# A two-layer transformer kernel: inverse head norms by ten operations for each sequence, and all first-layer rounds ordered ahead of all second-layer rounds

## The chip, the cores and the metric

The kernel runs on one core of one Trainium2 chip. The metric is the time on the device in microseconds (us) for one execution; lower is better. Times of a kernel are given as the median of several runs.

## The reference

Two transformer layers work on 8 sequences of 128 tokens with 256 channels, conditioned by one vector of 256 for each sequence.

```python
# first layer: 16 heads of 16
ada = silu(cond) @ Wada.T + bada            # gamma1, gamma2, scale1, scale2, shift1, shift2
q, k, v = split((ln(x) * (scale1 + 1) + shift1) @ Wqkv.T + bias)
qn = q / max(norm(q), 1e-12) * exp(min(scale_mul_log, log(100)))
kn = k / max(norm(k), 1e-12)
x = x + (softmax(qn @ kn.T + mask) @ v @ Wproj.T + bproj) * gamma1
x = x + (gelu_tanh((ln(x) * (scale2 + 1) + shift2) @ Wfc1.T + bfc1) @ Wfc2.T + bfc2) * gamma2
# second layer: 8 query heads of 32, one key and value head, rotary positions
h = ada_rms(x, cond, ln1_w, ln1_tw)
x = x + softmax(rope(h @ Wq.T) @ rope(h @ Wk.T).T / sqrt(32)) @ (h @ Wv.T) @ Wo.T
h = ada_rms(x, cond, ln2_w, ln2_tw)
x = x + (silu(h @ Wg.T) * (h @ Wu.T)) @ Wd.T
```

The hidden width of both MLPs is 1024.

## The kernel before, in words

**Tiling.** A token is a partition. A round is one pair of sequences in one layer; there are 4 pairs and 2 layers, so 8 rounds, listed in `ROUNDS` (line 57) as (pair, layer). The step number `n` is twice the round plus the sequence within the pair, and `j = n % 2` picks one of two buffers. Each round has an attention part ("a") and an MLP part ("m"). Products with Wqkv, Wfc1, Wq, Wkv, Wg and Wu are made from high and low parts in three matmuls (lines 1366 to 1368); ScalarE (ACT) makes the high part of the activations (line 944) and GpSimd (POOL) the low part (line 822).

**A first-layer attention, for each sequence.** `norm_stats` (VectorE, DVE), `norm_root` (POOL), `norm_apply` (DVE), a transpose on TensorE (PE), `norm_mod` and `norm_high` (ACT), `norm_low` (POOL), `qk_product` (PE), `qk_copy` (DVE, line 1155), `qk_square` (ACT, line 952) and `qk_sum` (DVE: the sum at line 1175, the floor at line 1180, and a first guess of the inverse root from the bits at lines 1185 and 1188). Then `qk_root` on POOL (lines 826 to 848) refines the guess, once for both sequences of the pair: one operation for minus half of the sum, three Newton steps of four operations on 128x64 values, and one that multiplies the q half by the head scale (line 847), 14 operations in all. `qk_scale` (DVE, line 1195) multiplies q and k by the result, `qk_high` (ACT, lines 960 and 961) and `qk_low` (POOL, lines 854 and 855) split them into half-precision parts, and `q_turn` and `k_turn` (PE, lines 1443 and 1452) transpose them, with copies on DVE. Four groups of four heads follow: `scores` (PE, line 1481), `mask_add` and `row_max` (DVE, lines 1254 and 1265), `exp` (ACT, line 980), `probs_turn` (PE, line 1497), `probs_copy` (ACT, line 1000), `values` (PE, line 1513). At the end stand `project` (PE, line 1532), `residual` (DVE, line 1308) and `residual_add` (POOL, line 884 times gamma, line 887 plus x).

**The rest.** A second-layer attention has two groups for each sequence (exp at line 984), normalised on POOL (line 874). A first-layer MLP has four chunks `fc1` (two sums on ACT at line 1019, then lines 1024, 1315, 1031 and 1324) and two `down` products (line 1562); a second-layer MLP has eight chunks `gate_up` with little ACT work and the same two `down` products.

**Order.** Nothing in the file lists the instructions. At build time `list_steps` writes each step with its engine, an assumed duration, what it comes after, and a priority put together from `ATT_BASE`, `MLP_BASE`, `SHIFT` and others; `make_orders` then plays these steps through with a greedy rule and so fixes the order in each engine's queue and the PSUM banks. An engine works its queue strictly in that order and waits where a semaphore isn't there yet. Where the plan sees PE idle, it puts in filler matmuls (`warm`, line 1396) that keep TensorE's clock up; they compute nothing. There is one PSUM bank for transposes ("turn"), one for linear products, two for hidden ones. Steps of one kind follow `n`: the norms, scores, projections and MLPs of a round come after those of the rounds ahead of it in `ROUNDS`; different kinds can overlap, so an MLP of one round runs beside the attention of another.

**Gammas.** The gammas of a pair go through a scratch tensor in memory and are loaded back by SyncE (line 777) into one of two buffers (pair % 2). The load for pair 2 waits until the first-layer MLP residual of pair 0 has been scaled, and that for pair 3 until that of pair 1 has been (line 884 releases it). `residual_add` on POOL waits for the gammas of its pair.

Of the kernel before, what the change touches and what calls it, by code (L numbers as in the profile page):

```python
# [28 lines left out]
ALU = mybir.AluOpType  # L29
# [3 lines left out]
P = 128  # L33
# [10 lines left out]
MAX_LOG_SCALE = float(np.log(np.float32(100.0)))  # L44
GELU_C = float(np.sqrt(2.0 / np.pi).astype(np.float32))
# [4 lines left out]
NEWTON = 3  # L50
# [24 lines left out]
for _i, _c in enumerate(CHUNKS):  # L75
# [14 lines left out]
SHIFT = {  # L90
    'warm': 900.0, 'angles': 925.5, 'attn_copy': 434.0, 'cond_silu': -640.5, 'cond_tanh': -405.5, 'down':
    947.5, 'exp': 360.0, 'fc1': -277.0, 'gamma_load': -658.5, 'gamma_store': 624.5, 'gate': -299.0,
    'gate_up': 365.5, 'gelu': -1217.0, 'gelu_in': 1213.0, 'gelu_inner': 16.5, 'head_clip': 1045.5,
    'head_exp': 500.5, 'inv_copy': 16.5, 'inv_spread': 490.5, 'inv_turn': 90.0, 'k_copy': -524.0, 'k_turn':
    -1072.5, 'load': -193.0, 'load_small': 627.0, 'load_whole': 1282.0, 'load_x': -159.5, 'mask_add':
    -171.0, 'modulate': 747.0, 'modulated': 9.5, 'norm_apply': -1665.5, 'norm_high': -1020.5, 'norm_low':
    -756.0, 'norm_mod': -339.0, 'norm_probs': -148.0, 'norm_root': 55.0, 'norm_stats': -323.5, 'norm_turn':
    -635.5, 'probs_copy': 382.0, 'probs_turn': -90.0, 'project': -100.0, 'q_copy': 132.0, 'q_turn': 98.0,
    'qk1_copy': 629.0, 'qk1_turn': -1542.5, 'qk_copy': 291.0, 'qk_high': 218.5, 'qk_low': -419.0,
    'qk_product': -509.5, 'qk_root': -297.5, 'qk_scale': -261.0, 'qk_square': -313.0, 'qk_sum': 49.0,  # L100
    'qkv1_copy': -1082.5, 'qkv1_product': 401.0, 'residual': -48.0, 'residual_add': 119.0, 'rope': 1132.5,
    'row_inverse': 1112.5, 'row_max': -1805.5, 'scores': -397.0, 'sines': 391.5, 'store': 1349.0,
    'sum_inverse': -962.0, 'tanh': -19.5, 'v_copy': -307.0, 'v_product': 1260.5, 'values': -69.5,
    'weight_high': 592.0, 'weight_low': 626.0, ('norm_stats', 'a'): 285.5, ('norm_stats', 'm'): -665.0,
    ('norm_root', 'a'): 136.0, ('norm_root', 'm'): -1064.0, ('norm_apply', 'a'): -644.5, ('norm_apply',
    'm'): -450.5, ('norm_turn', 'a'): -712.5, ('norm_turn', 'm'): 265.5, ('norm_mod', 'a'): -873.0,
    ('norm_mod', 'm'): 40.0, ('norm_high', 'a'): -363.0, ('norm_high', 'm'): -559.0, ('norm_low', 'a'):
    -278.5, ('norm_low', 'm'): 436.5, ('residual', 'a'): -248.5, ('residual', 'm'): -49.0, ('residual_add',
    'a'): 1035.0, ('residual_add', 'm'): 113.0}
# [17 lines left out]
LATENCY = 2.2  # L127
# [26 lines left out]
def list_steps():  # L154
# [39 lines left out]
    for i, name in enumerate(WHOLE):  # L194
        add(("load_whole", name), "SP", 0.75 if i < 2 else 3.0, [], at=0.0)
# [35 lines left out]
    for r, (pair, layer) in enumerate(ROUNDS):  # L231
# [4 lines left out]
        for j, n in enumerate(ns):  # L236
# [5 lines left out]
            if layer == 0:  # L242
                w_ready = ("weight_low", CHUNK_AT[("Wqkv", 2)])
                add(("qk_product", n), "PE", 1.55, [("norm_low", "a", n), w_ready], "linear", at=a)
# [3 lines left out]
                add(("v_product", n), "PE", 0.8, [("norm_low", "a", n), ("qk_product", n), ("weight_low", LAST_CHUNK["Wqkv"])], "linear", at=a + 0.1)  # L248
# [4 lines left out]
                if j == 1:  # L253
                    add(("qk_root", r), "Pool", 5.0, [("qk_sum", m) for m in ns] + [("head_exp",)], at=a)
                for m in ns if j == 1 else ():
                    b = base + 2 + 1.0 * (m % 2)
                    add(("qk_scale", m), "DVE", 0.6, [("qk_root", r)], at=b)
                    add(("qk_high", m), "ACT", 0.85, [("qk_scale", m), last_j.get(("kt", m % 2))], at=b)
                    add(("qk_low", m), "Pool", 1.75, [("qk_high", m)], at=b)
                    add(("q_turn", m), "PE", 0.53, [("qk_low", m)], "turn", at=b)  # L260
                    add(("q_copy", m), "DVE", 0.665, [("q_turn", m), last_scores], frees=("q_turn", m), at=b)
                    add(("k_turn", m), "PE", 0.25, [("q_turn", m)], "turn", at=b)
                    add(("k_copy", m), "DVE", 0.33, [("k_turn", m), last_scores], frees=("k_turn", m), at=b)
                    last_j[("qk", m % 2)], last_j[("pack", m % 2)], last_j[("kt", m % 2)] = (("qk_scale", m), ("qk_low", m),
                                                                                          ("k_turn", m))
            else:
                add(("qkv1_product", n), "PE", 1.0, [("norm_low", "a", n), ("weight_low", LAST_CHUNK["Wkv"])],
# [5 lines left out]
                add(("qk1_turn", n), "PE", 0.43, [("rope", n)], "turn", at=a)  # L273
# [33 lines left out]
            if layer == 0:  # L307
# [41 lines left out]
        for j, n in enumerate(ns):  # L349
# [4 lines left out]
                + ([("gamma_load", pair)] if layer == 0 else [])  # L354
# [132 lines left out]
def build(nc, x, columns, pos, mask, w, out):  # L487
    with ExitStack() as ctx:
# [52 lines left out]
        head_scale = sb("head_scale", [P, H0])  # L541
# [23 lines left out]
        qk_half = sb("qk_half", [P, 2, 2 * H0])  # L565
# [229 lines left out]
        def _(pool):  # L795
# [4 lines left out]
            pool.memset(minus_half[:, :], -0.5)  # L800
            pool.memset(v_pad[:, :, :, :], 0.0)
# [24 lines left out]
            def qk_root_(r):  # L826


                o = ord0(2 * r) // 2
                half, t, y = qk_half[:, :, :], qk_t[:, :, :], qk_r[:, :, :]  # L830
                done = o * 4 * NEWTON
                pool.wait_ge(qk_guess, 2 * o + 2)
                pool.tensor_scalar(half, qk_fl[:, :, :], -0.5, None, ALU.mult)
                for i in range(NEWTON):
                    if i:
                        pool.wait_ge(qk_root_step, done + 4 * i)
                    pool.tensor_tensor(t, y, y, ALU.mult).then_inc(qk_root_step, 1)
                    pool.wait_ge(qk_root_step, done + 4 * i + 1)
                    pool.tensor_tensor(t, t, half, ALU.mult).then_inc(qk_root_step, 1)
                    pool.wait_ge(qk_root_step, done + 4 * i + 2)  # L840
                    pool.tensor_scalar(t, t, 1.5, None, ALU.add).then_inc(qk_root_step, 1)
                    pool.wait_ge(qk_root_step, done + 4 * i + 3)
                    pool.tensor_tensor(y, y, t, ALU.mult).then_inc(qk_root_step, 1)
                pool.wait_ge(qk_root_step, done + 4 * NEWTON)
                if o == 0:
                    pool.wait_ge(scale_ready, 1)
                pool.tensor_tensor(qk_r[:, :, 0:H0], qk_r[:, :, 0:H0],
                                   head_scale[:, :].unsqueeze(1).to_broadcast([P, 2, H0]), ALU.mult).then_inc(qk_rnorm, 1)
# [768 lines left out]
```

## Time and profile before

| what | us |
|---|---|
| median of 3 runs (lowest, highest) | 340.05 (339.28, 344.35) |
| the profiled execution, its whole time | 337.69 |
| its span, first to last instruction | 335.9 |
| mean granted clock of TensorE in it | 0.98 of full speed |

The profile is of one execution. A group of instructions is named by its line in the kernel's file, its engine and its operation. "Busy" is the time in which an engine had an instruction under way; busy time of PE holds the filler matmuls too. "Idle before" is the time in which the engine stood still ahead of these instructions, with the instruction whose end released it.

### The profile page before, as it was taken

The page shows a single profiled execution, that of the slowest core. Times are in us where ns is not written, and L with a number is a line of the kernel's source. Part 1 is how long each engine was busy: PE and PEld are TensorE (multiplying, and loading weights), DVE is VectorE, ACT ScalarE, POOL GpSimd, SP SyncE. Part 2 cuts the span into 40 slices and gives each one's busy share as a digit, 9 for nine tenths or more (in the row PEclk, how much of TensorE's full clock was granted, in tenths as well). Part 3 has the DMA queues.
Part 4 walks back from the last instruction along what each step waited for, and adds up shares of the span by engine and source line. Part 5 has one row for each costly group of instructions (what it writes and reads, how often), then busy time and mean ns, then how long its engine had stood idle before and what let it go on. Part 6 is the DMA issues. An engine that isn't in the chain of part 4 may idle for free.

```text
span 335.9 us, 7317 instructions
## 1 busy us (share of the span) xinstructions
PE 301.0 (90%) x2516; PEld 251.2 (75%) x2516; DVE 221.2 (66%) x535; ACT 207.0 (62%) x698; POOL 149.7 (45%) x264
## 2 busy tenths in 40 slices
PE   7797766799987989986999999999979999999986
PEld 7396555576866866765797878889768898988985
DVE  3854788688777889858868688664453883543441
ACT  3454639989992899887699576836571433632110
POOL 3446959764475453688325138522214512202000
PEclk9599999999997999999999999999979999999999
DMA  6998223000000020000001000000000000000000
GB/s 200 283 338 283 83 92 126 1 2 3 1 2 2 0 65 0 3 1 3 0 2 64 0 2 2 2 0 18 8 12 0 2 0 18 17 2 19 16 0 33
DMA packets 14037, 14.30 MB, mean 43 GB/s; under 512 B 1569, under 2 KB 12961, under 8 KB 14001
## 3 DMA queue, kind: packets, MB, share of 16 engines
q1 hardware_dynamic: 14000, 13.83, 13.1%
q8 instruction: 21, 0.34, 0.4%
q14 instruction: 16, 0.12, 0.1%
HBM read 12.76 MB, written 1.06 MB: 41 GB/s over the span
## 4 chain that ended last, share of the span: by engine, by line
PE 54%; DVE 16%; POOL 9%; issue 8%; ACT 8%; DMA 3%; SPq 1%; DVEq 0%; POOLq 0%; ACTq 0%
PE ps_linear L1562 15%; PE ps_hidden L1366 6%; PE ps_hidden L1368 5%; PE ps_hidden L1367 5%; PE ps_linear L1532 3%; PE ps_probs L1497 3%; ACT z L980 3%; DMA stage<-in_Wqkv 3%; DVE z L1254 2%; PE ps_scores L1486 2%; PE ps_turn L1402 2%; DVE neg_max L1265 2%; PE ps_output L1513 2%; PE ps_turn L1396 1%; PE ps_scores L1481 1%
## 5 line engine op out<-in xcount | busy, mean ns | idle before, releaser
L980 ACT ACTIVATE z<-z,neg_max 128x128 f32<-128x128 f32 x128 | 49.6, 391 | 13.1 <-DVE neg_max L1265 12.9
L822 POOL TENSOR_TENSOR h_lo<-xn,h_hi 128x256 fp32r<-128x256 f32 x32 | 24.1, 756 | 40.9 <-ACT h_hi L944 40.8
L1000 ACT ACTIVATE probsT<-ps_probs 128x512 f32<-128x512 f32 x48 | 28.4, 591 | 11.3 <-PE ps_probs L1497 11.2
L1497 PE MATMUL ps_probs<-ident,z 128*128 128x128 f32 x192 | 29.9, 278 | 3.7 <-ACT probsT L1000 2.6
L1562 PE MATMUL ps_linear<-WdT,g_h 128*128 128x256 f32 x128 | 29.5, 383 | 1.4 <-DVE g_h L1337 1.3
L1036 ACT ACTIVATE g_a<-ps_hidden 128x256 f32<-128x256 f32 x32 | 12.4, 387 | 29.0 <-PE ps_hidden L1368 28.6
L874 POOL TENSOR_TENSOR z<-z,row_inv 128x512 f32<-128x512 f32 x16 | 17.0, 1062 | 28.1 <-DVE row_inv L1279 28.1
L1562 PE MATMUL ps_linear<-Wfc2T,g_h 128*128 128x256 f32 x128 | 29.4, 382 | 0.0
L1497 PEld LDWEIGHTS ps_probs<-ident,z 128*128 128x128 f32 x192 | 21.7, 141 | 7.7 <-ACT probsT L1000 3.7
L1562 PEld LDWEIGHTS ps_linear<-WdT,g_h 128*128 128x128 f32 x128 | 23.7, 190 | 5.0 <-issue 1.4
L984 ACT ACTIVATE z<-ps_scores,neg_max 128x128 f32<-128x128 f32 x64 | 22.6, 368 | 7.8 <-DVE neg_max L1271 7.8
L1562 PEld LDWEIGHTS ps_linear<-Wfc2T,g_h 128*128 128x128 f32 x128 | 23.8, 191 | 3.6 <-issue 0.2
L1254 DVE TENSOR_TENSOR z<-ps_scores,bias_mask 128x512 f32<-128x512 f32 x32 | 21.9, 683 | 5.1 <-PE ps_probs L1497 3.4
L884 POOL TENSOR_TENSOR res_t<-res_t,gamma 128x256 f32<-128x256 f32 x16 | 13.5, 846 | 24.9 <-DVE res_t L1308 24.9
L980 ACT ACTIVATION_READ_ACCUMULATOR z<-z,neg_max 128x1 f32 x128 | 24.2, 189 | 0.0
L1265 DVE TENSOR_REDUCE neg_max<-z 128x4 f32<-128x512 f32 x32 | 21.7, 679 | 1.1
L1332 DVE SCALAR_TENSOR_TENSOR g_b<-g_a,ps_hidden 128x256 f32<-128x256 f32 x32 | 13.4, 417 | 12.9 <-ACT g_a L1036 12.6
L1366 PE MATMUL ps_hidden<-h_hi,WgT_hi 128*128 128x256 f32 x64 | 21.0, 328 | 0.3 <-ACT g_u L1019 0.3
L1366 PE MATMUL ps_hidden<-h_hi,Wfc1T_hi 128*128 128x256 f32 x64 | 19.4, 302 | 0.0
L816 POOL TENSOR_TENSOR rstd<-msq,minus_half 128x1 f32<-128x1 f32 x32 | 18.1, 566 | 2.7
L1366 PE MATMUL ps_linear<-WqkvT_hi,h_hi 128*128 128x512 f32 (+1 forms) x32 | 12.3, 384 | 7.0 <-DVE qk L1155 2.9
L1366 PE MATMUL ps_hidden<-h_hi,WuT_hi 128*128 128x256 f32 x64 | 18.1, 283 | 0.0
(166 smaller groups left out, 897.5 us busy)
## 6 DMA issues: line engine op xcount, KB each, us to landing
gamma<-gamma_scratch SPq DMA_DIRECT2D x8, 256.0 KB, 3.8
stage<-in_Wada SPq DMA_DIRECT2D x6, 256.0 KB, 4.0
stage<-in_Wqkv SPq DMA_DIRECT2D x4, 256.0 KB, 4.9
X<-in_x SPq DMA_DIRECT2D x4, 256.0 KB, 5.3
stage<-in_Wfc SPq DMA_DIRECT2D x4, 256.0 KB, 5.8
Wfc2T<-in_Wfc SPq DMA_DIRECT2D x1, 1024.0 KB, 7.5
WdT<-in_Wd SPq DMA_DIRECT2D x1, 1024.0 KB, 8.5
stage<-in_Wg SPq DMA_DIRECT2D x4, 256.0 KB, 2.7
```

Source lines behind the costliest of these rows:

```text
L816: pool.tensor_tensor(rstd[:, k, :], msq[:, k, 1:2], minus_half[:, 0:1], ALU.pow).then_inc(rstd_ready[kind], 1)
L822: pool.tensor_tensor(h_lo[:, m, :, j * P:(j + 1) * P], h_full[:, m, j, :, :], h_hi[:, m, :, j * P:(j + 1) * P].bitcast(F32), ALU.subtract) ...
L874: pool.tensor_tensor(z[:, d, :, :], z[:, d, :, :], row_inv[:, d, :].unsqueeze(2).to_broadcast([P, 4, P]), ALU.mult).then_inc(probs_ready, 1)
L980: ins = act.activation(z[:, d, u, :], z[:, d, u, :], ACT.Exp, bias=neg_max[:, d, u:u + 1], accum_out=head_sum[:, n % 2, t, u, b:b + 1])
L984: ins = act.activation(z[:, d, u, :], ps_scores[u // 2][:, (u % 2) * P:(u % 2 + 1) * P], ACT.Exp, bias=neg_max[:, d, u:u + 1], accum_out=r ...
L1000: act.activation(probsT[:, G % 2, :, :], bank_of(key)[:, :].rearrange("p (u q) -> p u q", u=4), ACT.Copy).then_inc(is_freed(key)[0], 1)
L1254: ins = dve.tensor_tensor(z[:, G % DEEP, :, :], ps_scores[b][:, :].rearrange("p (u k) -> p u k", u=4), bias_mask[:, :].unsqueeze(1).to_bro ...
L1265: dve.tensor_reduce(neg_max[:, d, :], z[:, d, :, :], AX_X, ALU.max, negate=True).then_inc(max_ready, 1)
L1366: pe.matmul(dst, sh, mh, start=i == 0, stop=False)
L1367: pe.matmul(dst, sh, ml, start=False, stop=False)
L1497: ins = pe.transpose(bank[:, u * P:(u + 1) * P], z[:, G % DEEP, u, :], ident[:, :])
L1562: ins = pe.matmul(bank[:, 0:C], g_h[:, f, j * P:(j + 1) * P], WT1[name][:, f, :], start=(f == 0), stop=(f == FT - 1))
```

## The change

1. `ROUNDS` becomes all four first-layer rounds, then all four second-layer rounds; before, round 3 is the second layer of pair 0 and round 4 the first layer of pair 3.
2. `qk_root` runs once for each sequence on 128x32 values, in ten operations: one step of third order (six operations) and one Newton step (four). The head scale is folded in earlier: `head_exp` makes the exponential of minus twice the log scale, and the floor in `qk_sum` becomes one operation that also multiplies by it, so the inverse root comes out scaled. The buffer `qk_half` goes, `qk_u` comes.
3. The step list: assumed durations are other numbers, some steps come after other ones in the plan, every step of a kind comes after the one before it (a new loop at the end of `list_steps`), and all the priority numbers are others. So the order in every queue is another.

```diff
+MIN_LOG_SCALE = -20.0
-NEWTON = 3
-ROUNDS = [(0, 0), (1, 0), (2, 0), (0, 1), (3, 0), (1, 1), (2, 1), (3, 1)]
+ROUNDS = [(0, 0), (1, 0), (2, 0), (3, 0), (0, 1), (1, 1), (2, 1), (3, 1)]
...
-GROUP_US = [-39.5, -38.5]
-ATT_BASE = [-1173.0, 265.0, 221.5, -749.5, 36.5, 113.5, -2.0, 608.0]
-MLP_BASE = [58.5, 771.5, 12.5, -147.0, -1056.5, -973.5, -16.5, -206.0]
+GROUP_US = [-44.5, -668.5]
+ATT_BASE = [-4536.0, -432.5, 816.5, -3308.5, 363.5, -2581.0, 60.5, 745.5]
+MLP_BASE = [554.0, 3234.5, -2707.0, -1333.0, -1121.0, -4845.5, 1417.5, -1651.5]
...
-LATENCY = 2.2
+LATENCY = 3.0
...
-        add(("load", c), "SP", 0.75, [user] if c >= STAGE else [], at=due)
+        add(("load", c), "SP", 0.95, [user] if c >= STAGE else [], at=due)
...
-                add(("qk_sum", n), "DVE", 1.25, [("qk_square", n), last_j.get(("qk", j))], at=a)
+                add(("qk_sum", n), "DVE", 1.3, [("qk_square", n), ("head_exp",), last_j.get(("qk", j))], at=a)
+                add(("qk_root", n), "Pool", 3.5, [("qk_sum", n)], at=a)
+                add(("qk_scale", n), "DVE", 1.0, [("qk_root", n)], at=a)
...
-                    add(("qk_root", r), "Pool", 5.0, [("qk_sum", m) for m in ns] + [("head_exp",)], at=a)
...
-                    add(("qk_scale", m), "DVE", 0.6, [("qk_root", r)], at=b)
...
-            add(("project", n), "PE", 0.95, [("attn_copy", n), ("load_whole", "Wproj" if layer == 0 else "Wo"), prev(("project",), n)], "linear", at=g)
+            add(("project", n), "PE", 0.95, [("attn_copy", n), ("load_whole", "Wproj" if layer == 0 else "Wo"), prev(("project",), n)]
+                + ([("gamma_load", pair)] if layer == 0 else []), "linear", at=g)
...
+    last = {}
+    for key, step in steps.items():
+        name = key[:2] if len(key) > 2 and isinstance(key[1], str) else key[0]
+        if name not in ("load", "load_x", "load_whole", "gamma_load", "modulate", "modulated", "store"):
+            if name in last and last[name] not in step[2]:
+                step[2].append(last[name])
+            last[name] = key
...
+            pool.memset(head_scale[:, H0:2 * H0], 1.0)
...
+            def qk_root_(n):
+
+                o, j = ord0(n), n % 2
+                x, t, u, y = qk_fl[:, j, :], qk_t[:, j, :], qk_u[:, j, :], qk_r[:, j, :]
+                done = o * 9
+                pool.wait_ge(qk_guess, o + 1)
+                pool.tensor_tensor(t, y, y, ALU.mult).then_inc(qk_root_step, 1)
+                pool.wait_ge(qk_root_step, done + 1)
+                pool.tensor_tensor(t, t, x, ALU.mult).then_inc(qk_root_step, 1)
+                pool.wait_ge(qk_root_step, done + 2)
+                pool.tensor_scalar(u, t, 0.375, -1.25, ALU.mult, ALU.add).then_inc(qk_root_step, 1)
...
+                pool.tensor_tensor(y, y, t, ALU.mult).then_inc(qk_rnorm, 1)
...
-                act.activation(head_scale[:, :], head_log[:, :], ACT.Exp).then_inc(scale_ready, 1)
+                act.activation(head_scale[:, 0:H0], head_log[:, :], ACT.Exp, scale=-2.0).then_inc(scale_ready, 1)
...
-                    dve.wait_ge(qk_rnorm, o // 2)
-                dve.tensor_scalar(qk_fl[:, j, :], qk_ss[:, j, :], NORM_FLOOR, None, ALU.max).then_inc(qk_floored, 1)
+                    dve.wait_ge(qk_rnorm, o - 1)
+                if o == 0:
+                    dve.wait_ge(scale_ready, 1)
+                    dve.wait_ge(consts_set, 2)
+                dve.scalar_tensor_tensor(out=qk_fl[:, j, :], in0=qk_ss[:, j, :], scalar=NORM_FLOOR,
+                                         in1=head_scale[:, :], op0=ALU.max, op1=ALU.mult).then_inc(qk_floored, 1)
```

## Rows read from the trace of the kernel before

**Rows 1.** The page: busy time, and the span in 40 slices.

```profile
PE 301.0 (90%) x2516; PEld 251.2 (75%) x2516; DVE 221.2 (66%) x535; ACT 207.0 (62%) x698; POOL 149.7 (45%) x264
...
PE   7797766799987989986999999999979999999986
```

**Rows 2.** Busy time of every engine in five stretches (us, busy, and count).

```profile
core 0: us, PE busy (x) PEld busy (x) DVE busy (x) ACT busy (x) POOL busy (x), PEclk, DMA share, GB/s
0.00:80.00 80.00, 62.86 (x571) 50.61 (x572) 54.03 (x127) 51.63 (x165) 50.46 (x102) 0.96 0.48 148
80.00:140.00 60.00, 55.08 (x502) 42.48 (x501) 50.12 (x116) 49.35 (x179) 32.58 (x58) 0.97 0.04 11
140.00:200.00 60.00, 54.27 (x472) 45.65 (x470) 45.19 (x99) 46.70 (x155) 29.51 (x49) 1.00 0.03 10
200.00:300.00 100.00, 97.14 (x772) 83.53 (x771) 60.01 (x167) 53.83 (x189) 34.16 (x51) 0.98 0.02 7
300.00:336.00 36.00, 31.67 (x207) 28.89 (x206) 11.82 (x29) 5.53 (x15) 2.97 (x6) 1.00 0.05 16
```

**Rows 3.** The same stretches for the filler matmuls of line 1396 alone.

```profile
0.00:80.00 80.00, 25.00 (x174) 22.51 (x174) 0.96 0.48 148
80.00:140.00 60.00, 5.48 (x28) 4.56 (x28) 0.97 0.04 11
140.00:200.00 60.00, 3.79 (x22) 2.92 (x22) 1.00 0.03 10
200.00:300.00 100.00, 0.71 (x4) 0.52 (x4) 0.98 0.02 7
300.00:336.00 36.00, 4.86 (x32) 4.37 (x32) 1.00 0.05 16
```

**Rows 4.** Stretches from 49 us on: all engines (columns of rows 2), then line 980 alone.

```profile
49.00:136.00 87.00, 76.80 (x776) 59.52 (x776) 70.74 (x154) 75.79 (x286) 51.25 (x82) 0.98 0.06 19
...
49.00:136.00 87.00, 39.39 (x192) 0.98 0.06 19
136.00:163.00 27.00, 0.00 (x0) 1.00 0.01 2
163.00:200.00 37.00, 13.14 (x64) 1.00 0.05 16
```

**Rows 5.** Timeline from 24 to 41 us: start, us, instruction [idle before <-releaser].

```profile
24.06 0.18 DVE L1188 TENSOR_SCALAR qk_r<-qk_t 128x32 int32<-128x32 int32 x1
...
26.96 0.40 POOL L833 TENSOR_SCALAR qk_half<-qk_fl 128x64 f32<-128x64 f32 x1 [5.30 <-DVE qk_r L1188]
...
32.24 0.25 POOL L847 TENSOR_TENSOR qk_r<-qk_r,head_scale 128x32 f32<-128x32 f32 x1
...
32.52 2.90 DVE L1195 TENSOR_TENSOR qk_n<-qk,qk_r 128x512 f32<-128x512 f32 x2 [3.70 <-POOL qk_r L847]
...
40.07 0.82 DVE L1180 TENSOR_SCALAR qk_fl<-qk_ss 128x32 f32<-128x32 f32 x1
...
40.68 0.61 PE L1443 MATMUL ps_turn<-ident,qk_pack 128*128 128x128 f16 x8
```

**Rows 6.** The same view from 45 to 50 us.

```profile
46.43 0.62 PE L1481 MATMUL ps_scores<-qkT 32*128 32x128 f16 x16 [0.52 <-DVE qkT L1212]
```

**Rows 7.** Groups of instructions: line, shapes, count | busy, mean ns | idle before.

```profile
L1019 ACT ACTIVATE g_u<-ps_hidden,cols 128x256 f32<-128x256 f32 x32 | 13.3, 471 | 5.0 <-DVE g_h L1324 2.8 <-PE ps_hidden L1368 1.9
...
L1024 ACT ACTIVATE g_a<-g_u 128x512 f32<-128x512 f32 x16 | 10.1, 631 | 0.5
L1031 ACT ACTIVATE g_a<-g_a 128x512 f32<-128x512 f32 x16 | 10.0, 627 | 6.6 <-DVE g_a L1315 6.5
...
L847 POOL TENSOR_TENSOR qk_r<-qk_r,head_scale 128x32 f32<-128x32 f32 x4 | 1.0, 252 | 0.3
```

**Rows 8.** The tile qk_r: duration ns min/median/max.

```profile
L1195 DVE TENSOR_TENSOR qk_n<-qk,qk_r x8: 679/1208/1783, 32.5 to 150.1; 128x512 f32<-128x512 f32 x8
```

**Rows 9.** Timeline of SyncE, its own queue, from 110 to 190 us: start, us.

```profile
118.60 61.81 SPq L777 DMA_DIRECT2D gamma<-gamma_scratch  x4
```

More of the change, by code:

```diff
@@ L89 @@
-MLP_SPAN = [-295.5, 386.0]
+    'Wfc1': 3452.0, 'Wg': 6004.0, 'Wkv': 6995.5, 'Wq': 14980.0, 'Wqkv': 7580.0, 'Wu': 816.0, 'ada': 4153.0,
+    'tw1': -5640.0, 'tw2': -12260.0}
+MLP_SPAN = [-2417.5, 1856.0]
 SHIFT = {
[L91 to L109, printed above, removed]
@@ new lines @@
+    'warm': 900.0, 'angles': -1430.0, 'attn_copy': 1353.0, 'cond_silu': 1214.0, 'cond_tanh': -128.0, 'down':
+    2544.5, 'exp': 3590.5, 'fc1': -2119.5, 'gamma_load': -5297.5, 'gamma_store': 1271.5, 'gate': 1008.5,
+    'gate_up': 2148.0, 'gelu': -1431.5, 'gelu_in': 2821.5, 'gelu_inner': 3299.5, 'head_clip': -1007.0,
+    'head_exp': -86.5, 'inv_copy': 2411.0, 'inv_spread': 38.5, 'inv_turn': -608.5, 'k_copy': 913.0,
+    'k_turn': 182.5, 'load': -3058.0, 'load_small': -1827.0, 'load_whole': 1833.5, 'load_x': -3235.0,
@@ new lines @@
+    'mask_add': -3494.0, 'modulate': 4350.0, 'modulated': -4724.5, 'norm_apply': -6469.5, 'norm_high':
+    -2670.0, 'norm_low': 475.5, 'norm_mod': 2906.5, 'norm_probs': 2517.0, 'norm_root': 8164.0, 'norm_stats':
+    -6013.5, 'norm_turn': 1321.5, 'probs_copy': -3580.0, 'probs_turn': -952.5, 'project': 1303.5, 'q_copy':
+    -2100.0, 'q_turn': 5045.5, 'qk1_copy': 5160.0, 'qk1_turn': -4944.5, 'qk_copy': -2817.5, 'qk_high':
+    -4697.5, 'qk_low': -441.5, 'qk_product': -4609.0, 'qk_root': 2856.0, 'qk_scale': -2440.5, 'qk_square':
@@ new lines @@
+    -5053.0, 'qk_sum': 3466.5, 'qkv1_copy': -4366.5, 'qkv1_product': 3399.0, 'residual': -2000.5,
+    'residual_add': -1035.0, 'rope': 516.5, 'row_inverse': 3166.5, 'row_max': -3801.5, 'scores': -2664.0,
+    'sines': 633.0, 'store': 5604.0, 'sum_inverse': -3480.5, 'tanh': 1721.5, 'v_copy': -5454.5, 'v_product':
+    1661.5, 'values': 84.5, 'weight_high': -1160.0, 'weight_low': 1142.5, ('norm_stats', 'a'): 1017.5,
+    ('norm_stats', 'm'): 45.5, ('norm_root', 'a'): -1427.5, ('norm_root', 'm'): -2154.0, ('norm_apply',
@@ L112, in CHUNK_DUE @@
+    'a'): -4212.0, ('norm_apply', 'm'): -1619.0, ('norm_turn', 'a'): -1912.5, ('norm_turn', 'm'): -1839.5,
+    ('norm_mod', 'a'): -477.0, ('norm_mod', 'm'): -2547.0, ('norm_high', 'a'): 449.5, ('norm_high', 'm'):
+    -1547.0, ('norm_low', 'a'): -1036.0, ('norm_low', 'm'): 1027.0, ('residual', 'a'): 3694.5, ('residual',
+    'm'): -2722.0, ('residual_add', 'a'): 3695.0, ('residual_add', 'm'): 631.5}
 def CHUNK_DUE(c):
@@ L243, in list_steps @@
                 w_ready = ("weight_low", CHUNK_AT[("Wqkv", 2)])
-                add(("qk_product", n), "PE", 1.55, [("norm_low", "a", n), w_ready], "linear", at=a)
+                add(("qk_product", n), "PE", 1.55, [("norm_low", "a", n), w_ready, last_j.get(("qk", j))], "linear", at=a)
                 add(("qk_copy", n), "DVE", 0.6, [("qk_product", n), ("load_small",), last_j.get(("qk", j))], frees=("qk_product", n),
@@ new lines, in list_steps @@
+                add(("qk_root", n), "Pool", 3.5, [("qk_sum", n)], at=a)
+                add(("qk_scale", n), "DVE", 1.0, [("qk_root", n)], at=a)
+                add(("qk_high", n), "ACT", 0.85, [("qk_scale", n), last_j.get(("kt", j))], at=a)
+                add(("qk_low", n), "Pool", 1.75, [("qk_high", n)], at=a)
+                add(("q_turn", n), "PE", 0.53, [("qk_low", n), last_scores], "turn", at=a)
+                add(("q_copy", n), "DVE", 0.665, [("q_turn", n), last_scores], frees=("q_turn", n), at=a)
@@ L266, in list_steps @@
+                add(("k_turn", n), "PE", 0.25, [("q_turn", n)], "turn", at=a)
+                add(("k_copy", n), "DVE", 0.33, [("k_turn", n), last_scores], frees=("k_turn", n), at=a)
+                last_j[("qk", j)], last_j[("pack", j)], last_j[("kt", j)] = (("qk_scale", n), ("qk_low", n),
+                                                                              ("k_turn", n))
+                ready = ("k_copy", n)
             else:
-                add(("qkv1_product", n), "PE", 1.0, [("norm_low", "a", n), ("weight_low", LAST_CHUNK["Wkv"])],
+                add(("qkv1_product", n), "PE", 1.0, [("norm_low", "a", n), ("weight_low", LAST_CHUNK["Wkv"]), last_values],
@@ L353, in list_steps @@
             add(("residual", "m", n), "DVE", 0.335, [("down", n), prev(("residual", "m"), n)]
-                + ([("gamma_load", pair)] if layer == 0 else [])
                 + ([("residual_add", "m", q) for q in (n - 1,) if ("residual_add", "m", q) in steps]),
@@ L824, in norm_low @@
                                    ALU.subtract).then_inc(h_low[kind], 1)
[L826 to L848, printed above, removed]
```

55 lines of the change are left out of this document (27 added, 28 removed).

## The prediction

> **What bounds the kernel now.** I read the page first: PE is busy 90% of the span, and its row of tenths is ragged in the first half and almost full from slice 21 on [rows 1]. Part of that busy time is filler, so I took the stretches and subtracted the filler matmuls [rows 2, 3]. What is left is real PE work:
>
> - 0 to 80 us: 62.86 - 25.00 = 37.86
> - 80 to 140: 55.08 - 5.48 = 49.60, a share of 0.827
> - 140 to 200: 54.27 - 3.79 = 50.48, 0.841
> - 200 to 300: 97.14 - 0.71 = 96.43, 0.964
> - 300 to 336: 31.67 - 4.86 = 26.81
>
> The sum is 261.2 us of real work in 335.9. So some 75 us are lost, 42 of them before 80 us, 20 between 80 and 200, 4 between 200 and 300, 9 in the tail. The kernel is bound by PE only from 200 us on. Before that it waits for the first attention to get going, and then for ACT and DVE: from 49 to 136 us, the three first-layer attentions of pairs 0 to 2, ACT is busy 75.8 of 87 us (0.87) and DVE 70.7 (0.81), while POOL has 36 us free [rows 4]. The exponentials of line 980 show the order: 192 instructions in those 87 us, none from 136 to 163 while the second layer of pair 0 goes first, the last 64 after 163 [rows 4].
>
> **The change, part by part.** There are four terms: the round order, the root, POOL and its port, the plan.
>
> *Round order.* Three first-layer attentions take 87 us, 29 each, and the first exponential starts with that stretch, at 49. With pair 3 right behind pair 2 the fourth ends near 136 + 29 = 165 and not at 200. Up to 80 us both orders hold the same rounds: 37.9 us of work. From 80 to 165 I keep the share of 0.827: 85 x 0.827 = 70.3, together 108.2. Left are 153.0. The tail of 36 us holds 26.8 of it as now; the other 126.2 run in a stretch in which the second-layer rounds are all still to come. These ask little of ACT (54 of 100 us) and DVE (60 of 100) [rows 2], so I take the share of 200 to 300: 126.2 / 0.964 = 130.9. End: 165 + 130.9 + 36 = 331.9 us of span, 4 less than now. The bounds: if the first 35 us behind 165 keep 0.841, since two or three first-layer MLPs are then still open, 35 x (0.964 - 0.841) / 0.964 = 4.5 us are lost again; if the share between 80 and 165 rises to 0.91 because more MLP work lies beside the attention, 85 x 0.083 / 0.964 = 7.3 are won. I take 0, which is nearest to the rows that stand.
>
> *The root, at the start.* The guess for sequence 0 is there at 24.06 + 0.18 = 24.2, but the pair's root waits for sequence 1 and starts at 26.96, after POOL had idled 5.30 us; it ends at 32.49 and DVE scales at 32.52 [rows 5]. That is 5.53 us for 14 operations, 0.40 each. On 32 columns the one such operation takes 0.25 [rows 7], with the same gap some 0.34. Ten make 3.4 to 4.0 us: sequence 0 is scaled at about 28, 4.2 earlier, sequence 1 near 32, where now the second of the two scalings ends at 35.4. But behind the scaling the way is not clear: q is only transposed at 40.68 [rows 5], the first scores come at 46.43 [rows 6], 14 us after the scaling, through POOL's queue of weight splits and the one transpose bank. If only the root's 4.2 us pass, the start moves by 4; if the queue behind it clears as well, scores can start near 34.5 and 12 us are won; if POOL's new order puts splits ahead of the roots, it is 2 us later. I take 5, nearest to the root's own 4.2. Until 80 us the engines wait on this start, so it counts in full.
>
> *The root, later.* A pair now costs POOL 2 x 3.4 to 2 x 4.0 = 6.8 to 8.0 us in place of 5.5, 5 to 10 us in all. POOL's 36 idle us from 49 to 136 cover that; without that cover it is the 10. DVE's floor becomes a two-input operation of the same 32 columns; below I put nothing, above the 0.82 us that the stretched one took, 6.6 us for eight. I take nothing, since the unstretched ones beside it took 0.18. DVE waits once for the head scale; behind that wait the next `qk_copy` and the modulation copies are queued, and PE's linear bank behind `qk_copy`. Exponential and table load take under 2 us on ACT, which has time there: nothing, at worst 2.
>
> *POOL's port.* DVE is slowed where POOL works. The scaling of line 1195 takes between 679 and 1783 ns for one shape [rows 8], and the floor at 40.07, on 32 columns, takes 0.82 us [rows 5]. Twenty small POOL operations for a pair in place of 14, with DVE at 0.81, give more such meetings: 24 more, each of at most one POOL operation of 0.25, is 6 us; at best none meets. I take 1: POOL has over a third of that stretch idle, and many of the meetings fall where DVE waits anyway. The Trainium skill, page "SBUF — State Buffer", section "Who interferes with whom", says that DVE and GpSimd share one port pair as an exclusive lock and that the second to ask waits for the whole instruction of the first. The rows on line 1195 agree with it; by that rule alone, all 24 meeting, the sum would be 5 us higher than mine, and with no meeting 1 us lower.
>
> *The plan.* Its new durations are nearer to this trace: `qk_scale` 1.0 for a measured median of 1.2, where it stood at 0.6 [rows 8]. That favours an order whose waits come as planned, but I have no row that prices it: 0, between the bounds of the share above. SyncE's queue keeps its loads; the weights are in long before the second layer, and only its gamma loads can block (below). The fillers follow the plan and fill only idle time.
>
> *Sum.* 331.9 - 5 + 1 = 327.9 us of span. The profiled execution was 337.69 for a span of 335.9, so 1.8 lie around it: 329.7. The median of the runs is 2.36 above that execution: 332.1, so **332.0 us**, 2.4% below 340.05. A measurement tells about 2% from no change, here 333.2 to 346.9.
>
> **Rivals.**
>
> *No gain.* First-layer rounds are heavy for ACT: their MLP costs it (13.3 + 10.1 + 10.0) / 4 = 8.4 us a round beside the attention [rows 7]. The stretch from 49 to 136 holds only one such MLP, 8.4 / 0.87 = 9.6 us of its 87; without it an attention takes 25.8 and a round with its MLP 35.4. If the MLPs of pairs 1 and 2 are put beside the attentions and PE's share does not rise with them, but falls to 0.75, an estimate between the 0.47 of the first 80 us and the 0.827, 85 x 0.077 / 0.964 = 6.8 us are lost, and the start gives nothing (+5): 327.9 + 11.8 = 339.7, and 4.2 for median and surroundings: **344**. Against it speaks that MLP work is PE work. That the change does less than it says belongs here: only steps of one kind are bound to the round order, the rest mixes as before.
>
> *Slower.* The gammas have two buffers. Those of pair 3 are loaded when the first-layer MLP residual of pair 1 has been scaled: SyncE waits 61.8 us for it, until 180.4 [rows 9]. Now pair 3's projection comes only afterwards and nobody minds. In the new order its attention ends near 160, and the new plan also puts `project` behind that load. If the MLP of pair 1 is as late as now, pair 3's `residual_add` stands in POOL's queue, and behind it the norms, low parts and normalised probabilities of the second layer, for 180.4 - 160, some 20 us in which PE soon has nothing ready: 327.9 + 20 + 4.2 = **352**; with 4 us of it covered by an MLP, 348. It decides from about 15 us of stall (332 + 15 = 347). For it speaks that the priority number of that MLP is late (3234.5); against it that its input, pair 1's attention, is done well before 136, when the exponentials of all three pairs end [rows 4], and that PE has free time from then on.
>
> *Much faster.* The start's 12 us instead of 5 and the share of 0.91: 327.9 - 7 - 7.3 + 4.2 = **318**; half of both, 325.
>
> **How the numbers follow.** The forecast has 0.50, with a range of its own from 324 to 339; two thirds of it lie below 333.2. No gain 0.19, slower 0.21 (348 to 352), much faster 0.10. Faster by over 2%: 0.33 + 0.10 = 0.43; within 2%: 0.17 + 0.19 = 0.36; slower: 0.21. The range for 8 in 10 is 319 to 350: it takes in the bounds of the unknown costs and the near half of the slow case.
>
> **What would show it.** The first scores near 41 us and not 46; the last exponential of line 980 near 160 and not 200, with no gap in between; ten operations of a quarter of a microsecond for each root; real PE work of about 100 us or more by 160; PE above 0.95 from there to the tail. Wrong would be: a long idle of POOL before line 884 near 160 to 180, first scores still at 46 or later, a PE share well under 0.9 behind the last line 980, or DVE's small operations much longer than before.

## The result, and the profile after

The changed kernel takes **330.69 us** (median of 4 runs, 329.41 to 331.48) beside 341.21 us for the kernel before (4 runs, 339.28 to 344.35): a ratio of 0.968 with a 95% interval of 0.959 to 0.977. Forecast were 332.0 us, in a range of 319 to 350, from three runs of the kernel before with a median of 340.05; the fourth moved that median to 341.21. The time is right; two of the terms behind it are not, and they offset each other.

The profiled execution took 331.48 us for a span of 329.4. The page, with busy time and the same row of tenths as in [rows 1]:

```profile
PE 300.3 (91%) x2494; PEld 252.2 (77%) x2494; DVE 220.9 (67%) x535; ACT 205.9 (63%) x698; POOL 155.7 (47%) x289
...
PE   6999878899887998899898999899999989999996
...
PEclk9697899999997999999999999999999999999999
```

Busy time by stretch (columns as in [rows 2]), then the fillers alone, now of line 1406 (as in [rows 3]):

```profile
0.00:80.00 80.00, 69.79 (x612) 56.30 (x613) 61.75 (x157) 58.41 (x193) 55.35 (x135) 0.91 0.49 148
80.00:160.00 80.00, 71.66 (x674) 57.02 (x674) 66.84 (x139) 67.69 (x232) 48.91 (x82) 0.98 0.05 15
160.00:200.00 40.00, 37.28 (x310) 30.96 (x309) 22.20 (x58) 30.53 (x102) 20.02 (x28) 1.00 0.01 2
200.00:300.00 100.00, 95.32 (x729) 83.53 (x728) 61.72 (x163) 46.20 (x165) 31.44 (x45) 1.00 0.02 7
300.00:330.00 30.00, 26.22 (x178) 24.39 (x176) 8.34 (x20) 3.07 (x8) 0.00 (x0) 1.00 0.05 18
```

```profile
0.00:80.00 80.00, 22.14 (x128) 19.74 (x129) 0.91 0.49 148
80.00:160.00 80.00, 4.42 (x30) 3.71 (x29) 0.98 0.05 15
160.00:200.00 40.00, 1.95 (x13) 1.70 (x14) 1.00 0.01 2
200.00:300.00 100.00, 6.17 (x40) 5.21 (x40) 1.00 0.02 7
300.00:330.00 30.00, 4.32 (x30) 3.94 (x30) 1.00 0.05 18
```

Real PE work is the difference: 47.7 us by 80 us, where it was 37.9 [rows 2, 3]; then 67.2 of 80 us, 35.3 of 40, 89.2 of 100 (it was 96.4) and 21.9. The sum is 261.3, before it was 261.2. Busy time stretches where the clock is low: the eight transposes of q at 34.40, in the timeline below, took 0.97 us at a mean granted clock of 0.61 (32 to 36 us), and the same eight at 40.68 in the kernel before 0.61 us at 1.00 (40 to 44 us) [rows 5]. The mean clock of the first 80 us is 0.91 here and was 0.96, so the count of instructions tells it better: 612 - 128 = 484 real matmuls by 80 us in place of 571 - 174 = 397. By 200 us the changed kernel is 12.3 us of work ahead, at 300 only 5.0 (239.4 beside 234.4), and it ends 6.5 us of span earlier.

The first root, from the timeline of 20 to 45 us; it answers to [rows 5, 6]:

```profile
22.50 0.18 DVE L1198 TENSOR_SCALAR qk_r<-qk_t 128x32 int32<-128x32 int32 x1
...
22.77 0.24 POOL L836 TENSOR_TENSOR qk_t<-qk_r 128x32 f32<-128x32 f32 x1 [4.29 <-DVE qk_r L1198]
...
25.80 0.25 POOL L854 TENSOR_TENSOR qk_r<-qk_r,qk_t 128x32 f32<-128x32 f32 x1
...
26.11 1.17 DVE L1205 TENSOR_TENSOR qk_n<-qk,qk_r 128x512 f32<-128x512 f32 x1
...
34.40 0.97 PE L1453 MATMUL ps_turn<-ident,qk_pack 128*128 128x128 f16 x8
...
37.88 0.62 PE L1491 MATMUL ps_scores<-qkT 32*128 32x128 f16 x16 [0.34 <-DVE qkT L1222]
```

The root runs from 22.77 to 26.05, 3.28 us for ten operations, and the first scores come at 37.88 in place of 46.43. The exponentials of the first layer, their durations and first and last start:

```profile
L986 ACT ACTIVATE z<-z,neg_max x128: 384/394/425, 41.2 to 159.7; 128x128 f32<-128x128 f32 x128
```

They run from 41.2 to 159.7 without the gap of before, where they went from 49.1 to 199.4 [rows 4]. The gammas of pair 3 wait until 128.23 + 27.72 = 155.95 and not 180.4 [rows 9]:

```profile
128.23 27.72 SPq L780 DMA_DIRECT2D gamma<-gamma_scratch  x4
```

### The profile page after: what moved, and what is told of

Its sections match the earlier page's. It is cut to its first block, busy times and chain, and to the rows that moved or that the text cites. A ratio compares the mean times of both kernels' runs of the same rounds, so it can differ in the third digit from the quotient of the medians.

```text
span 329.4 us, 7305 instructions
## 1 busy us (share of the span) xinstructions
PE 300.3 (91%) x2494; PEld 252.2 (77%) x2494; DVE 220.9 (67%) x535; ACT 205.9 (63%) x698; POOL 155.7 (47%) x289
## 4 chain that ended last, share of the span: by engine, by line
PE 48%; DVE 20%; POOL 11%; ACT 10%; issue 7%; DMA 2%; SPq 1%; DVEq 0%; ACTq 0%; POOLq 0%
PE ps_linear L1572 14%; PE ps_hidden L1376 5%; PE ps_hidden L1378 4%; PE ps_hidden L1377 4%; ACT z L986 3%; DVE z L1264 3%; DVE neg_max L1275 3%; PE ps_scores L1406 2%; PE ps_scores L1496 2%; PE ps_probs L1507 2%; PE ps_linear L1542 2%; PE ps_output L1523 2%; ACT z L990 2%; PE ps_linear L1376 2%; PE ps_turn L1412 1%
## 5 line engine op out<-in xcount | busy, mean ns | idle before, releaser
L1042 ACT ACTIVATE g_a<-ps_hidden 128x256 f32<-128x256 f32 x32 | 12.3, 386 | 41.0 <-PE ps_hidden L1378 39.6
L1572 PE MATMUL ps_linear<-Wfc2T,g_h 128*128 128x256 f32 x128 | 29.6, 384 | 0.7 <-ACT qkv L977 0.7
L986 ACT ACTIVATION_READ_ACCUMULATOR z<-z,neg_max 128x1 f32 x128 | 25.0, 195 | 0.0
L1342 DVE SCALAR_TENSOR_TENSOR g_b<-g_a,ps_hidden 128x256 f32<-128x256 f32 x32 | 13.4, 418 | 15.7 <-ACT g_a L1042 15.2
L1264 DVE TENSOR_TENSOR z<-ps_scores,bias_mask 128x512 f32<-128x512 f32 x32 | 21.9, 683 | 2.0 <-PE ps_scores L1491 1.0
L1312 DVE TENSOR_TENSOR X<-ps_linear,X 128x256 f32<-128x256 f32 x16 | 6.8, 422 | 22.3 <-PE ps_linear L1572 20.1
L820 POOL TENSOR_TENSOR rstd<-msq,minus_half 128x1 f32<-128x1 f32 x32 | 19.4, 606 | 2.7
L818 POOL TENSOR_SCALAR msq<-msq 128x1 f32<-128x1 f32 x16 | 4.5, 281 | 32.9 <-DVE msq L1137 32.7
L950 ACT ACTIVATE h_hi<-xn 128x256 fp32r<-128x256 f32 x32 | 13.2, 416 | 10.4 <-PE ps_hidden L1378 6.6
```

Of the source, the lines that this page charges most:

```text
L820: pool.tensor_tensor(rstd[:, k, :], msq[:, k, 1:2], minus_half[:, 0:1], ALU.pow).then_inc(rstd_ready[kind], 1)
L986: ins = act.activation(z[:, d, u, :], z[:, d, u, :], ACT.Exp, bias=neg_max[:, d, u:u + 1], accum_out=head_sum[:, n % 2, t, u, b:b + 1])
L1264: ins = dve.tensor_tensor(z[:, G % DEEP, :, :], ps_scores[b][:, :].rearrange("p (u k) -> p u k", u=4), bias_mask[:, :].unsqueeze(1).to_bro ...
L1342: dve.scalar_tensor_tensor(out=g_b[:, f % 2, 0:256], in0=g_a[:, f % 2, 0:256], scalar=1.0, in1=bank_of(key)[:, 0:256], op0=ALU.add, op1=AL ...
L1572: ins = pe.matmul(bank[:, 0:C], g_h[:, f, j * P:(j + 1) * P], WT1[name][:, f, :], start=(f == 0), stop=(f == FT - 1))
```

## The experiments

**1. One part at a time, with every queue left as it was.** Three kernels keep their parent's queues, step for step, and alter the root only. The fourth moves the second layer of pair 0 ahead of the first layer of pair 3 again and lets the plan be made anew.

The old root in the changed kernel's order: the pair root of before, its 14 operations on 128x64, at the even sequence's place, with the head scale and the floor as before too.

```diff
-            def qk_root_(n):
+            def qk_root_(r):
...
+            def qk_root_pair(n):
+                if n % 2 == 0:
+                    qk_root_(n // 2)
```

> The changed kernel with every queue in its own order, and only the root as before: one root of 14 operations for a pair, at the place of the even sequence, where it waits for the guess of the odd one too. Theory A (the root's shorter way at the start is a good part of the gain): the first root begins near 24.4 instead of 22.8 and ends near 29.9 instead of 26.0, the first scores move from 37.9 to about 41 to 42, and the time rises by 3 to 5 us from 330.7 to about 335. Rival B (the gain is the order's, the root only rides along): first scores move, but the time rises by under 1.5 us.

Measured: **345.58 us** (4 runs; 1.015 of the kernel before, 1.009 to 1.021), 14.9 above the changed kernel. Neither number was right: the direction was A's, the size three times its upper 5 us. Its waits, and its first-layer scores and exponentials with first and last start:

```profile
  POOL qk_r L851: 13.7, 4
```

```profile
L1489 PE MATMUL ps_scores<-qkT x256: 211/214/225, 42.8 to 169.5; 32*128 32x128 f16 x128
```

```profile
L988 ACT ACTIVATE z<-z,neg_max x128: 384/392/420, 46.0 to 175.0; 128x128 f32<-128x128 f32 x128
```

DVE now stands 13.7 us for the root, in four waits of up to 5 us; in the changed kernel it was 2.0. The first scores are late by 42.8 - 37.9 = 4.9 us, as expected. Of these, 1.1 lie ahead of the root: the guess starts at 23.64 where it started at 22.50. But the last exponential starts at 175.0 and not 159.7, so 10 us more are lost inside the stretch of the four attentions. The delay grows from round to round: the even sequence's guess is late by 1.1, 4.4, 5.6 and 10.0 us in the four. Each round pays, not the first one alone.

The root's length is only part of that. At the even sequence's place the pair root also waits for the guess of the odd one, which comes 1.7, 3.6, 4.8 and 1.8 us later in the four rounds, 11.9 in all; its operations take 5.5 us in place of 3.3, which is 9 in all. POOL works its queue in order, so all that stands behind the root waits too. The third round shows it (start, us, instruction, idle before):

```profile
83.31 0.40 POOL L837 TENSOR_SCALAR qk_half<-qk_fl 128x64 f32<-128x64 f32 x1 [6.29 <-DVE qk_r L1196]
...
88.77 0.40 POOL L872 COPY wide_inv<-head_inv 128x256 f32<-128x256 f32 x1
88.85 0.85 DVE L1203 TENSOR_TENSOR qk_n<-qk,qk_r 128x512 f32<-128x512 f32 x1 [5.04 <-POOL qk_r L851]
...
89.22 0.69 PE L1530 MATMUL ps_turn<-ident,wide_inv 128*128 128x128 f32 x2 [6.02 <-POOL wide_inv L872]
```

POOL stands 6.29 us for the odd guess, DVE 5.04 for the root, and PE 6.02 us for a copy of inverse row sums (`wide_inv`) of the attention before, which stood behind the root in POOL's queue. In the changed kernel PE never waits for that copy.

The clock falls too. The stretch from 80 to 100 us in this kernel, and in the changed one:

```profile
core 0: us, PE busy (x) PEld busy (x) DVE busy (x) ACT busy (x) POOL busy (x), PEclk, DMA share, GB/s
80.00:100.00 20.00, 13.26 (x124) 11.06 (x119) 8.81 (x21) 13.10 (x47) 12.12 (x23) 0.83 0.00 1
```

```profile
80.00:100.00 20.00, 17.45 (x184) 14.08 (x184) 15.00 (x25) 18.46 (x57) 16.37 (x22) 1.00 0.00 1
```

PE has 13.3 busy us in place of 17.5, and the mean granted clock of these 20 us is 0.83; over the span it is 0.955 beside 0.974. Two of its stretches of 4 us, one within that wait and the next, show PE standing still and the clock falling behind it:

```profile
84.00:88.00 4.00, 0.00 (x0) 0.00 (x0) 0.00 (x0) 1.15 (x4) 3.21 (x10) 0.71 0.00 0
88.00:92.00 4.00, 2.78 (x13) 2.79 (x14) 1.63 (x4) 1.21 (x3) 1.78 (x5) 0.50 0.00 0
```

The new root in the order of before: both roots of a pair one behind the other at the pair root's place.

```diff
+            def qk_root_pair(r):
+                qk_root_(2 * r)
+                qk_root_(2 * r + 1)
```

> The kernel before with every queue in its own order, and only the root changed: two roots of ten operations for each pair at the pair root's place. Theory A: sequence 0's root begins at about 24.3 instead of 26.96, its scaling comes 4 us earlier, but the transposition at 40.7 waits for other things (the one transpose bank, weight splits), so first scores stay within 2 us of 46.4 and the time within 2 us of 340. Rival (the root alone makes the gain): first scores near 41 and 335 us or less.

Measured: **336.97 us** (9 runs), 0.992 of before (0.989 to 0.994), so 3 us faster. The scaling of sequence 0 starts earlier, at 29.6, but the first scores do not:

```profile
L1493 PE MATMUL ps_scores<-qkT x256: 212/214/309, 46.2 to 185.7; 32*128 32x128 f16 x128
```

So the root's shorter way is lost in the old queues: 46.2 where it was 46.4. What it brings there is about 1% of the time.

Ten more operations in each root:

```diff
+                for i in range(10):
+                    pool.wait_ge(qk_root_step, done + 9 + i)
+                    pool.tensor_tensor(u, t, t, ALU.mult).then_inc(qk_root_step, 1)
```

> The changed kernel with ten further chained POOL operations of the same size in each root, 0.33 us each, so 3.3 us more latency for each of eight sequences and 26 us more of POOL. If the roots sit on the path at the start alone: about +3 to +5 us, near 335. If POOL's time or its port to DVE matters in the first-layer stretch: +8 us or more. If POOL's idle time covers it all: under +1.5.

Measured: **353.64 us** (4 runs; 1.040 of before, 1.035 to 1.045), 23 above the changed kernel. The third expectation had the size but named POOL's time or its port as the cause. The rows tell the port from the rest:

```profile
L1208 DVE TENSOR_TENSOR qk_n<-qk,qk_r x8: 736/1416/1731, 28.2 to 143.7; 128x512 f32<-128x512 f32 x8
...
  POOL qk_r L857: 22.9, 7
```

DVE waits 22.9 us for the root, seven times, against 2.0 in the changed kernel. The scaling that meets POOL's operations grows from a median of 1144 ns to 1416, its eight together from 9.3 to 10.6 us, and all of DVE's busy time from 220.9 to 222.7. So the price is that the scaling comes later, in every round, and the port is a small part of it. Whether it comes later by the root's own length or because POOL is taken, the run does not separate: 15.8 of the 22.9 us are waits for the odd sequence, whose root stands in POOL's queue behind the longer one of the even sequence.

The round order with the same priority numbers:

```diff
-ROUNDS = [(0, 0), (1, 0), (2, 0), (3, 0), (0, 1), (1, 1), (2, 1), (3, 1)]
+ROUNDS = [(0, 0), (1, 0), (2, 0), (0, 1), (3, 0), (1, 1), (2, 1), (3, 1)]
-ATT_BASE = [-4536.0, -432.5, 816.5, -3308.5, 363.5, -2581.0, 60.5, 745.5]
+ATT_BASE = [-4536.0, -432.5, 816.5, 363.5, -3308.5, -2581.0, 60.5, 745.5]
...
```

> The changed kernel with the second layer of pair 0 ahead of the first layer of pair 3 again, each round keeping its priority numbers; the plan is made anew, so many queue places move. If the round order is worth the 4 us of the prediction: 334 to 338. If the priority numbers, found for another list, fit it badly: 340 or more, and this run then tells of the numbers and not of the rounds. If the round order is worth nothing: 331 within 2.

Measured: **329.55 us** (4 runs; 0.968 of before, 0.963 to 0.974), level with the changed kernel. With the old rounds the exponentials run until 190, not 160:

```profile
L986 ACT ACTIVATE z<-z,neg_max x128: 384/392/413, 39.1 to 189.9; 128x128 f32<-128x128 f32 x128
```

The kernel has lost nothing by it, so the 4 us that the forecast gave to the round order are not seen here. Its stretch from 200 to 300 us, and the fillers in it:

```profile
200.00:300.00 100.00, 98.17 (x750) 85.92 (x750) 56.57 (x154) 49.82 (x169) 29.92 (x45) 1.00 0.02 8
```

```profile
200.00:300.00 100.00, 3.98 (x26) 3.40 (x26) 1.00 0.02 8
```

That is 94.2 us of real PE work where the changed kernel does 89.2. What the changed kernel gains by having all first layers done at 160, it gives back later.

**2. A table of four, each corner with an order of its own.** A fixed order favours the root it was made for. So I took the changed kernel's list of steps, with the root old or new and the rounds old or new, and searched the priority numbers again by the same rule of chance, for each corner with the same effort. The plan's length by the changed kernel's durations was the goal; an old root counted 5.55 us for a pair. No computation is left out in any of them.

```diff
-ATT_BASE = [-4536.0, -432.5, 816.5, -3308.5, 363.5, -2581.0, 60.5, 745.5]
+ATT_BASE = [...]
-SHIFT = {'warm': 900.0, 'angles': -1430.0, ...}
+SHIFT = {...}
```

> The list of steps with the changed kernel's durations and chain, but the rounds of before and the pair root of before; its priority numbers searched anew, from nothing, with the same effort as the three runs beside it (some 174,000 plans each). This is the corner of a table of four: root old or new, rounds old or new. Theory A (root is worth much, rounds little): about 340, equal to q2 within 1.5%. Theory B (rounds are worth some 4 us by themselves): 4 us above q2.

> Pair root of before, all first-layer rounds first, numbers searched from nothing. Theory A (root): near 340, some 8 us above q4. Theory B (rounds): about 336, 4 us below q1 and near q4. If a search of this effort scatters by more than either effect, the four differ without a pattern.

> Root for each sequence, rounds of before, numbers searched from nothing. Theory A (root): near 331 to 334, 5 to 9 us below q1, as q4. Theory B (rounds): near q1, and 4 us above q4.

> Both changes, as the changed kernel, but numbers searched from nothing. It says how far another search of the same list lands from 330.7: within 1.5% if the time hangs on root and rounds, more than 2% off if it hangs on the numbers found.

The first table looked clean: 7.6 and 6.5 us for the root, 5.7 and 4.6 for the rounds. q4 is 1.1% from the changed kernel, within its expected 1.5%; q2 has the root theory's 340; q1 is 5.7 above q2 where the rounds' theory had 4; q3, 7.6 below q1 and 4.6 above q4, fits half of each. Since one search for each corner says nothing of its scatter, I made it a second time, from the changed kernel's numbers:

> The same table of four a second time, each corner now searched from the changed kernel's numbers instead of from nothing, with about 184,000 plans each. Both root and rounds old. If the table of q1 to q4 holds (root 6.5 to 7.6 us, rounds 4.6 to 5.7, additive): the slowest of the four, 10 us or more above p4. If it was scatter of the search: anywhere, also below p2. The plan puts it at the level of p3, which speaks for scatter in part; on the chip 338 to 342.

> Pair root, new rounds. Root theory: 7 us above p4, about 338. If the round order has a worth of its own: 5 us below p1.

> Root for each sequence, old rounds; without any search this combination took 329.6. If the round order has a worth of its own of some 5 us: 5 above p4. If r4 was the rule: level with p4, 328 to 331, and the rounds are worth nothing.

> Both new, the changed kernel's numbers refined a little further. 329 to 331, since its plan is shorter by only 0.3 us than that of the changed kernel.

| root, rounds | searched from nothing | searched from the changed kernel's numbers |
|---|---|---|
| old, old | 346.46 | 336.99 |
| old, new | 340.76 | 347.16 |
| new, old | 338.87 | 339.78 |
| new, new | 334.27 | 330.87 |

(Medians of 4 or 10 runs; the kernel before had 340.12 and 340.01 beside them.)

The second table breaks the first. Only p4's time came as expected; p1 is below p2, which its expectation had named as a mark of scatter, p2 is 9 us above its 338, and p3 is 8.9 above p4 where 5 or nothing was expected. The same corner differs by up to 9.5 us (q1 and p1) from one search to the next, and the new root with the old rounds took 338.87, 339.78 and, without any search, 329.55. Read by pairs, the rounds give 5.7, 4.6, -10.2 and 8.9 us, a mean of 2.3, and r4 against the changed kernel -1.1: no worth can be read from that. The root gives 7.6, 6.5, -2.8 and 16.3, a mean of 6.9, three of four with the same sign. That points to a gain; with a range that wide neither it nor its size is shown by the table.

What sets these orders apart shows in the start. First and last start of the first-layer exponentials for q4, p4 and p3, each from its own trace:

```profile
L965 ACT ACTIVATE z<-z,neg_max x128: 384/393/427, 34.7 to 165.3; 128x128 f32<-128x128 f32 x128
```

```profile
L965 ACT ACTIVATE z<-z,neg_max x128: 384/399/432, 40.5 to 159.2; 128x128 f32<-128x128 f32 x128
```

```profile
L965 ACT ACTIVATE z<-z,neg_max x128: 385/399/446, 45.3 to 199.1; 128x128 f32<-128x128 f32 x128
```

q4 starts 6 us before p4 and ends 6 later: an early start is not yet a gain. p3 and r4 have the same root and rounds; their starts are 6 us apart (45.3 and 39.1), their times 10. Up to 80 us p3 is not behind in real work (49.5 us beside 48.2). It loses from 80 to 200 us, as its stretches there show, and its fillers:

```profile
80.00:160.00 80.00, 72.93 (x602) 61.33 (x602) 61.65 (x131) 63.87 (x210) 53.86 (x85) 0.94 0.06 18
160.00:200.00 40.00, 35.40 (x337) 28.30 (x336) 30.92 (x73) 28.14 (x103) 17.80 (x33) 1.00 0.05 15
```

```profile
80.00:160.00 80.00, 11.67 (x60) 10.02 (x60) 0.94 0.06 18
160.00:200.00 40.00, 5.32 (x36) 4.66 (x36) 1.00 0.05 15
```

Real PE work is 61.3 + 30.1 = 91.4 of 120 us; r4 has 97.1 and the changed kernel 102.6. Which waits of that stretch are its cause was not taken apart.

## Why the prediction was right or wrong

**What bounds the kernel** held: the loss sat before 200 us, and there the gain came.

**The root at the start: mechanism right, the term mis-sized.** I took 5 us between -2 and 12; the first scores moved by 8.55. The parts: the guess comes 1.6 us earlier (22.68 for 24.24), from guess to scaling it is 3.4 us in place of 8.3, and from scaling to scores 11.8 in place of 13.9. The first of these may be luck: in r3, the changed kernel and r1, which have one and the same order, the guess starts at 21.5, 22.5 and 23.6. The root's own 3.28 us was forecast as 3.4 to 4.0. The order's part, that the queue behind the root clears, I had as a bound and not as the likely case. The new root alone moves the scores by 0.2 us (r2, 46.2), the new order alone by 3.6 (r1, 42.8), both together by 8.55.

**The root, later: the step that failed.** The forecast had nothing for the later roots, covered by POOL's free time. POOL's busy time rose by 6.0 us (149.7 to 155.7), inside the forecast 5 to 10, and was covered. But I priced POOL's load and not DVE's wait: with the old root in the new order the three later rounds cost 10 us more, beyond the start's 4.9. The time at which the root is done stands on the path in every first-layer round of this order, for DVE and for all that is queued behind it on POOL, and what I called covered is the larger part of that 14.9. POOL's idle time was no cover: part of it in r1, 18.6 us, is POOL itself standing in its queue for the guesses, 8.6 in the changed kernel. In the order of before the root was hidden for the most part: r2 gains only 3 us from the shorter one. So the parts do not add up one by one. The new order with the old root is 5.5 us slower than the kernel before, the new root in the old order 3 faster, both together 10.5 faster.

**POOL's port** was 1 us in the sum and is about nothing. The scaling's median is 1144 ns where it was 1208 [rows 8], all of DVE's busy time 220.9 us where it was 221.2 [rows 1], and 80 more POOL operations in r3 added 1.8 us to it. The floor as one two-input operation cost nothing either:

```profile
L1189 DVE SCALAR_TENSOR_TENSOR qk_fl<-qk_ss,head_scale x8: 191/192/241, 22.1 to 113.8; 128x32 f32<-128x32 f32 x8
```

The rule of the Trainium skill, page "SBUF — State Buffer", section "Who interferes with whom", agrees with the scatter of the scaling, 673 to 1632 ns in this trace; the sum by all meetings, 5 us more, was not seen.

**The round order: right by two errors.** The fourth attention was forecast to end near 165 or, with the early start, 160; the last exponential starts at 159.7. From there I took the share of 200 to 300 of the old trace, 0.964. Measured from 160 to 300 are (35.33 + 89.15) / 140 = 0.889. At that share the forecast's 126.2 us behind the attention take 142 and not 131, an error of 11.1 us. It was offset in part since by 160 us 114.9 us of real work were done, where the forecast had 108.2 (its value for 165, moved ahead by the 5 us of the start): the start gave more, and the share from 80 to 160 was 0.84. At 0.964 those 6.7 us are worth 7.0. So 327.9, less 7.0, plus the 142.0 - 130.9 = 11.1 and less 1 for the port, would be 331.0. Of the 1.6 us from there to 329.4, 0.6 are that with more done by 160 a shorter stretch ran at the low share (6.7 / 0.889 - 6.7 / 0.964); the rest I cannot place. The step from span to median was luck as well: I added 2.36 us because the median before stood that far above the profiled execution, and here it stands 0.8 below it, since the profiled one was the slowest of the four. It hides that the span came out 1.5 us longer than forecast. The old trace had its 0.964 with first-layer work of pair 3 kept until behind 163, some of it beside second-layer MLPs; r4 keeps it too and has 0.942 from 200 to 300. What stands in the way with all first layers in front, the chain of waits suggests; here it is for the changed kernel from 200 us on (start, us, what):

```profile
199.96 0.44 DVE res_t L1318
200.47 1.12 POOL res_t L890
201.66 1.07 POOL X L893
202.76 0.44 DVE stats L1130
...
205.23 1.14 POOL rstd L820
...
207.13 0.45 DVE rope_c L1234
207.58 0.99 DVE rope_s L1238 x2
209.22 0.61 DVE g_h L1334
210.20 0.44 ACT qkv L977
210.68 3.72 PE ps_linear L1572 x16
```

It is a chain of small steps, residual, gamma, statistics, norm, rotation, and at its end ACT copies a second-layer product out of the one linear bank at 210.20, so that the sixteen `down` matmuls start at 210.68. The second layer of the later pairs hangs on the last first-layer MLPs, and there is no attention of the first layer left to fill the time. That reading is argued from the chain; no run took it apart alone.

**The slower rival** did not come about. The plan put the MLP of pair 1 in front of pair 3's projection, the gammas came at 156, and no wait of POOL's line 890 is for them: its 27.0 us of idle time are all for DVE's residual.

**No gain and much faster.** The rival that the first-layer block thins PE out did not come: 0.84 where it would be 0.75. The one bound of the fast case, a start 12 us earlier, is more than reached by q4 (31.2 for the first scores, 15.2 earlier), at 334.3 us.

The claim in "the plan" that better durations favour an order whose waits come as planned stands open. p3's plan was 1.0 us shorter than r4's (330.3 and 331.2 by each kernel's own durations) and took 10 us longer.

## What to carry to other kernels

Price a latency where the queue's order has been made to fit it. An order planned around a 3.5 us step for each sequence loses at every round when the result comes later, be it that the step takes longer or that it waits for a second input, and what is queued behind it on its own engine loses as well, while that engine's busy share stays under one half. An order planned around 5 us gained only 3 us of 340 when the step took 3.3. When a change comes together with a new order, one search for each variant settles nothing: make a second one, and take the difference between the two as the error before reading any effect. And a share taken from one stretch of a trace belongs to the mix of work in that stretch; if the change takes that mix away, the share goes with it.

## What was not expected of the hardware

The granted clock fell behind a wait of a few us. In r1 PE did nothing from 84 to 88 us, and from 88 to 92 the clock was 0.50, the lower of its two levels (1.2 GHz); a 128x256 product matmul took 0.41 us there and 0.28 us at full clock in the changed kernel at 22 us. From 92 to 96 the mean was 0.94 and from 96 on 1.00. Over the whole span the clock was 0.955 in r1, 0.951 in r3, 0.974 in the changed kernel and 0.984 in r4. Taken by themselves, 0.974 - 0.955 over 344 us are 6.5 us at full clock, so some of r1's 14.9 may be clock and not wait; the runs do not separate the two.

A high busy share did not keep the clock up everywhere. In the changed kernel PE was busy 3.71 of the 4 us from 24 to 28 and all of the 4 from 28 to 32, and the clock of the second stretch was 0.54. Of the 33 matmuls from 24 to 28 us, 24 were small ones of line 1396 (outputs of 128x8). Why the clock fell was not taken apart.
